# Attention scores of 16 narrow heads: from full-array contraction to two 64-row tiles of the tensor engine

## The reference

```python
# layer 0, cross attention: 248 keys (128 of the side input, 120 of the context)
q = (x1 @ Wq + bq).reshape(Bn, Nq, 16, 8).transpose(0, 2, 1, 3)
k = concat([x2 @ Wk + bk, memory_k]);  v = concat([x2 @ Wv + bv, memory_v])
attn = softmax(einsum('bhqd,bhkd->bhqk', q, k) * 8 ** -0.5)
out = einsum('bhqk,bhkd->bhqd', attn, v) ... @ Wp + bp
# layer 1, self attention: 128 keys, rotary q and k, causal mask, same 16 heads of 8
```

## Time and profile before

| what | value |
|---|---|
| median of the runs | 3703.39 us (3702.83 to 3703.52) |
| span of the profiled execution | 3703.9 us |
| PE, PEld busy | 3561.7, 3078.1 us |
| DVE, ACT, POOL busy | 2874.9, 2007.9, 1379.6 us |
| cross stage, steady | about 645 to 1573 us |
| self stage, steady | about 2390 to 2975 us |
| granted PE clock | 0.98 of full on average, 1.00 inside both narrow stages |

### The profile page before, as it was taken

The page is one execution under the profiler, slowest core; times in us unless marked ns, Lnnn a source line. Parts: engine busy times, 40 slices in busy tenths (PEclk is TensorE's granted clock), DMA queues, the critical chain, the costliest instruction groups (busy, mean ns, idle before and its releaser), DMA issues. The chain is left out here.

```text
span 3703.9 us, 96400 instructions
## 1 busy us (share of the span) xinstructions
PE 3561.7 (96%) x29010; PEld 3078.1 (83%) x29010; DVE 2874.9 (78%) x8338; ACT 2007.9 (54%) x7830; POOL 1379.6 (37%) x3847
## 2 busy tenths in 40 slices
PE   6999998999999999989999999899999989999996
PEld 5888887888888888879999999788888868888884
DVE  3777776788787888778888888677777748888887
ACT  3656664666666666622222222277777746666663
POOL 1444444444444444300000000266666624444443
PEclk8999998999999999999999999999999989999998
DMA  3000000000000000000000000000000000000000
GB/s 110 23 23 22 23 22 26 24 23 23 23 21 24 21 21 24 12 12 11 11 11 10 11 10 11 14 23 21 21 21 21 20 26 26 25 25 25 25 23 11
DMA packets 166102, 81.63 MB, mean 22 GB/s; under 512 B 19536, under 2 KB 164304, under 8 KB 165968
## 3 DMA queue, kind: packets, MB, share of 16 engines
q1 hardware_dynamic: 165968, 79.98, 7.5%
HBM read 58.94 MB, written 20.97 MB: 22 GB/s over the span
## 5 line engine op out<-in xcount | busy, mean ns | idle before, releaser
L1068 ACT ACTIVATE pr<-psS,small 128x248 f32<-128x248 f32 (+1 forms) x2048 | 838.3, 434 | 510.7 <-DVE small L1158 473.4
L1158 DVE TENSOR_REDUCE small<-psS 128x4 f32<-128x992 f32 (+1 forms) x384 | 461.1, 1201 | 215.5 <-PE psS L1030 211.9
L1283 PE MATMUL psS<-experts_xT,e 128*128 128x256 f32 x2304 | 551.4, 382 | 0.0
L1317 ACT ACTIVATE experts_th<-psS 128x512 f32<-128x512 f32 x288 | 171.9, 597 | 603.1 <-PE psS L1283 603.1
L1030 PE MATMUL psS<-cross_qk,cross_Qx 128*128 128x248 f32 x2048 | 478.8, 373 | 0.0
L1283 PEld LDWEIGHTS psS<-experts_xT,e 128*128 128x128 f32 x2304 | 416.6, 191 | 48.0
L1068 ACT ACTIVATION_READ_ACCUMULATOR pr<-psS,small 128x1 f32 x2048 | 450.7, 220 | 0.0
L985 PE MATMUL psW<-ident,pr 128*128 128x128 f32 (+1 forms) x3072 | 420.7, 280 | 5.6 <-ACT pr L1068 5.2
L985 PEld LDWEIGHTS psW<-ident,pr 128*128 128x128 f32 (+1 forms) x3072 | 328.7, 140 | 84.5 <-ACT pr L1068 44.2
L1030 PEld LDWEIGHTS psS<-cross_qk,cross_Qx 128*128 128x128 f32 x2048 | 365.4, 191 | 28.8
L819 POOL TENSOR_SCALAR pr<-pr,small 128x128 f32<-128x128 f32 (+1 forms) x1024 | 357.6, 368 | 36.4 <-DVE small L762 30.2
(11 more groups left out here) (247 smaller groups left out, 7597.0 us busy)
## 6 DMA issues: line engine op xcount, KB each, us to landing
between<-self_xo SPq DMA_DIRECT2D x128, 64.0 KB, 1.6
cross_x<-between SPq DMA_DIRECT2D x128, 64.0 KB, 1.8
cross_res<-between SPq DMA_DIRECT2D x128, 64.0 KB, 1.8
cross_cx<-in_ctx SPq DMA_DIRECT2D x128, 60.0 KB, 1.9
self_x<-in_x SPq DMA_DIRECT2D x64, 64.0 KB, 1.8
self_res<-in_x SPq DMA_DIRECT2D x64, 64.0 KB, 1.8
cross_fs<-in_fside_BxSxS SPq DMA_DIRECT2D x64, 64.0 KB, 1.9
between<-cross_xo SPq DMA_DIRECT2D x64, 64.0 KB, 1.6
```

Source lines behind the costliest of these rows:

```text
L1068: last = act.activation(pr[e.slot % 4][:, cols], K.S[e.slot % 2][:, cols], ACT.Exp, bias=nmax[e.slot % 4][:, n:n + 1], accum_out=tot[k.slo ...
L1158: dve.tensor_reduce(nmax[u.slot % 4][:], src[:, :, 0:keys], AX.X, ALU.max, negate=True).then_inc(maxed, 1)
L1283: last = pe.matmul(K.S[u.slot % 2][:, at0 + blk * T:at0 + (blk + 1) * T], w[:, j, blk * P:(blk + 1) * P], xT[i.slot][:], start=True, stop= ...
L1317: act.activation(th[u.slot % 2][:], K.S[u.slot % 2][:, 0:2 * T], ACT.Tanh, scale=0.5).then_inc(tanhed, 1)
```

## The change

Heads 0 to 7 lie on rows 0 to 63, heads 8 to 15 on rows 64 to 127. The score matmul of a head now reads only the 64 rows that hold it, of the masked q and of k. A 64-row operand uses half of the matmul array's rows: rows 0 to 63 are one row tile, rows 64 to 127 the other. Since a head needs only its half, one masked copy can hold two heads, h and h+8, and `Qx` and the mask have 8 entries instead of 16. The heads of a unit are put in order by half: the first half of a unit (one PSUM bank) comes from the upper row tile, the second half (the other bank) from the lower. `S_ps` now counts twice a unit, once for each tile. `turn_sums` is called behind all scores of the step instead of behind the first head's.

```diff
     def heads(j):
-        return [4 * g + m for m in range(j * per_unit // 4, (j + 1) * per_unit // 4) for g in range(4)]
+        ms = range(j * per_unit // 4, (j + 1) * per_unit // 4)
+        return [4 * g + m for a in range(2) for m in ms for g in (2 * a, 2 * a + 1)]
...
-        Qx = [sb(f"Qx{i}", [P, NH, P]) for i in range(2)]
+        Qx = [sb(f"Qx{i}", [P, NH // 2, P]) for i in range(2)]
...
                         for n, h in enumerate(heads(j)):
-                            if n == 1:
-                                turn_sums(u - 3)
-                            last = pe.matmul(K.S[u.slot % 2][:, n * wide:n * wide + keys], Qx[i.slot % 2][:, h, :],
-                                             qk[i.slot][:, P:P + keys], start=cross,
+                            rows = slice(64 * (h // 8), 64 * (h // 8) + 64)
+                            last = pe.matmul(K.S[u.slot % 2][:, n * wide:n * wide + keys], Qx[i.slot % 2][rows, h % 8, :],
+                                             qk[i.slot][rows, P:P + keys], start=cross,
                                              stop=cross or n % 4 == 3)
-                        last.then_inc(S_ps, 1)
-                    else:
-                        turn_sums(u - 3)
+                            if n % (per_unit // 2) == per_unit // 2 - 1:
+                                last.then_inc(S_ps, 1)
+                    turn_sums(u - 3)
...
                     if u.live:
-                        need(dve, S_ps, u.done())
+                        need(dve, S_ps, u.done(2))
...
                     if b.live:
-                        for h in heads(j):
+                        for h in heads(j)[0:per_unit // 2]:
                             last = pool.tensor_scalar(Qx[b.slot % 2][:, h, :], qk[b.slot][:, 0:P], K.headmask[:, h:h + 1],
```

More of the change, by code:

```diff
@@ L133, in allocate @@
     K.causal = K.sb("causal", [P, 4 * P], BF16)
-    K.headmask = K.sb("headmask", [P, NH])
+    K.headmask = K.sb("headmask", [P, NH // 2])
     K.rope = K.sb("rope", [P, 4 * P])
@@ L1042, in step @@
                             h, c = (heads(tj)[n // 2], n % 2) if cross else (heads(tj)[n], 0)
-                            first = tj == 0 and (n % 2 == 0 if cross else n < 4)
-                            final = tj == units - 1 and (n % 2 == 1 if cross else n >= 4)
+                            first = tj == 0 and (n % 2 == 0 if cross else n % 4 < 2)
+                            final = tj == units - 1 and (n % 2 == 1 if cross else n % 4 >= 2)
                             size = chunks[c][1]
@@ L1101, in step @@
                             need(dve, proj_ps, b.done())
-                            need(dve, S_ps, (b - 4).done(units))
+                            need(dve, S_ps, (b - 4).done(2 * units))
                             need(dve, masked, (b - 4).done(units))
@@ L1144, in step @@
                             if cross:
-                                need(dve, S_ps, (a - 4).done(units))
+                                need(dve, S_ps, (a - 4).done(2 * units))
                                 dve.tensor_copy(qk[a.slot][:, 2 * P:2 * P + CTX], W[2][:, 3 * P:3 * P + CTX])
@@ L1186, in step @@
                         need(pool, proj_sb, b.done())
-                        need(pool, S_ps, (b - 2).done(units))
+                        need(pool, S_ps, (b - 2).done(2 * units))
                     if j == 0 and n.live:
@@ L1462, in constants @@
         "c_causal": np.where(rel > 0, f(-255 * 2.0 ** 120), f(0)).astype(f),
-        "c_headmask": (np.arange(P)[:, None] // HD == np.arange(NH)[None, :]).astype(f),
+        "c_headmask": (np.arange(P)[:, None] % 64 // HD == np.arange(NH // 2)[None, :]).astype(f),
         "c_rope": np.ascontiguousarray(np.concatenate([spin[0] * gain, spin[0], spin[1] * gain, spin[1]], 1)),
```

## The result

| | before | changed |
|---|---|---|
| median of the runs | 3703.11 us (3702.83 to 3703.52) | 3730.45 us (3728.08 to 3733.61) |
| ratio, 95% interval | | 1.0076 [1.0062, 1.0090] |
| span of the profiled execution | 3703.9 us | 3729.1 us |
| cross item | 14.55 us | 14.16 us |
| self item | 9.20 us | 10.05 us |

The median of the kernel before is now that of four executions; of the three known ahead of the prediction it was 3703.39 us. The interval of the ratio lies wholly above 1, so the kernel is slower, by less than 1%.

A forecast was written before the change was run, and what follows sets the result against it. PE was taken to bound both stages, with a chain through DVE binding the cross stage after the change. Self stage +47 and cross stage -22 made +25: 3703.4 + 25 = 3728 us, range 3684 to 3762 us.

The forecast's parts named there:

- The scores: Score matmuls on PE: 1.14 instead of 1.76 us a unit in the cross stage, 1.74 instead of 1.88 in self.
- both gaps: Changes of tiling before and after a unit's cross-stage scores: 0.09 us of PE time each.
- The set-up's eight matmuls over 64 rows: Set-up trace used as model for self-stage scores: 1.34 us from first pass to start of the last.
- rival D: Row tiles run in order, one pass overlapping; nothing gained in cross scores, 0.08 us more in self; 3839 us, 6%.
- The stall: PE waits for DVE's oT ahead of the weighted sums, once an item in both stages: +0.83 us.
- the +47 of the sum: Self stage, bound by PE: items from 9.20 to 9.90 us, +45 us over 64, +47 with small waits.
- the chain of 14.17: Cross stage: chain through DVE, PE and ACT binds the item at 14.17, 14.2 us with slack; -22 us over 64 items.
- DVE's fixed order carries it on: Cross stage: projections and inputs of other items precede the maxima on DVE; only 0.35 of 2.5 us freed reaches the item.
- B: Second tile starts at once in the self stage too: scores 1.19 us, item 9.2 us; 3681 us, 13%.
- C: PE stays the cross stage's bound, DVE catching up behind the stall: item 13.0 us, about 3651 us, 8%.
- POOL's zero: POOL's 8 fewer masked copies an item change nothing, as masks are done an item ahead: zero, bounds 0 and 0.
- The register instructions added on DVE: Extra waits on S_ps, about four per cross item on DVE: 0 to 0.4 us an item, value 0.

The follow-up runs named there:

- experiment 4: Changed kernel with turn_sums called ahead of the step's scores and heads issued alternately from the two row tiles: 3599.14 us, ratio 0.9714.
- experiment 3: Changed kernel with a unit's heads issued alternately from the upper and lower row tile, turn_sums still late: 3677.41 us, ratio 0.9930.
- experiment 5: Changed kernel with all score matmuls on rows 0 to 63, one row tile instead of two: 3949.48 us, ratio 1.0660.
- Experiment 9: Changed kernel without DVE's four small context copies in the cross stage: 3728.97 us; also with ACT's copies one exponential later in one step: 3707.74 us.
- experiment 1: Changed kernel with turn_sums called ahead of the step's scores, in the self stage behind the causal mask: 3627.69 us, ratio 0.9795.
- experiment 7: Changed kernel with POOL writing 16 masked copies an item again, PE reading only eight: 3731.13 us, ratio 1.0074.
- experiment 8: Changed kernel, heads alternating, turn_sums right behind the probabilities' transposes, DVE's copy and multiplication ahead of the projections: 3592.57 us; run again, 3592.74 us.

## Why the prediction was right

**The scores.** Right in both stages. Predicted with both gaps 1.14 us in the cross stage, measured 0.10 + 1.04; in the self stage 1.74, measured 0.10 + 1.64 (2650.67 to 2652.31 in the rows below; the two mask passes take 0.43 us to a group of their own tiling in experiment 4, so they end at 2650.57). The set-up's eight matmuls over 64 rows were a fair sample of what 16 self passes would do, and experiment 3 shows that the late start of the second tile is a matter of issue order.

```profile
2650.14 0.60 PE L1027 MATMUL psS<-causal,identb 128*128 128x512 bf16 x2
2650.67 1.71 PE L1031 MATMUL psS<-self_qk,self_Qx 64*128 64x128 f32 x16
2652.31 0.66 PE L1049 MATMUL psW<-self_pT,self_Vx 128*32 128x128 f32 x16
```

Strict order of all matmuls, rival D, is out: it left nothing to gain in the cross stage, and experiment 5, where tiles cannot overlap, is 219 us over the changed kernel. The Trainium skill, page "TensorE: Matmul & The Clock Gate", section "Part 3: Packing small matmuls", says that matmuls start and end strictly in program order. The measurements disagree across the two row tiles: the sixteen self passes take 1.64 us, where rival D had 1.87 for them without the gap, and the set-up's row at 29.44 starts ahead of three matmuls issued before it.

**The stall.** Right in place and cause, a little small. Predicted +0.83 us over the gap, from 0.16 + 0.04 + 0.67 + 0.05; from the transpose's start to the weighted sums the sum made 0.06 + 0.27 + 0.04 + 0.67 + 0.05 = 1.09, the traces show 1.20 in both stages. These rows of DVE in the changed kernel hold the parts:

```profile
1004.36 0.29 DVE L1123 COPY cross_invT<-psW 128x128 f32<-128x128 f32 x1 [0.98 <-PE psW L976]
1004.76 0.29 DVE L1126 TENSOR_TENSOR cross_oT<-psW,cross_invT 128x128 f32<-128x128 f32 x1
1004.97 1.18 DVE L1160 TENSOR_REDUCE small<-psS 128x4 f32<-128x992 f32 x1
```

DVE takes 0.69 and not 0.67, and from its end (1005.05) to PE's start (1005.19) are 0.14 and not 0.05. That 0.11 an item is 7 us in the self stage, where PE is the bound: +53.9 instead of the +47 of the sum.

**The cross stage.** Right in size (-25.2 against -22, item 14.16 against 14.2), and right that the gain ends in another chain than PE's. But its terms did not all come out. The same item's later rows of DVE:

```profile
1007.63 0.29 DVE L1134 TENSOR_TENSOR cross_yb<-cross_res,rowb 128x128 f32<-128x128 f32 x1 [0.39 <-PE psW L1017]
...
1009.32 1.16 DVE L1160 TENSOR_REDUCE small<-psS 128x4 f32<-128x992 f32 x1
...
1011.05 0.34 DVE L1107 TENSOR_SCALAR cross_qk<-psW,xb 128x128 f32<-128x128 f32 x1
...
1012.30 1.18 DVE L1160 TENSOR_REDUCE small<-psS 128x4 f32<-128x992 f32 x1
```

Maxima and copies take 1.73 us (9.32 to 11.05) and not 1.93, projections 1.25 and not 1.35. In the rows of before both ended with DVE running idle, so I had counted their last instruction to its end, and an instruction right behind it starts about 0.1 us sooner; the copies had also started 0.10 us later, when PE's transposes were through. On the other side DVE's input work starts 0.36 us behind the last input transpose's pass (1007.27 to 1007.63) and not 0.20, which it is in most other items, the last maxima to the first exponential take 1.30 (1012.30 to 1013.60) and not 1.23, ACT takes 2.60 from there to the transposes (1013.60 to 1016.20) and not 2.54, and the stall was 0.11 dearer. With these the chain of 14.17 becomes 14.27 or 14.28, which is this item's length. So the rows add up to the item along this chain, but the sum made ahead of them was close because errors of 0.3 us one way and 0.4 the other nearly cancel, and that is luck.

What the sum missed altogether is the chain that runs beside it, from the maxima of an item's last unit through ACT, PE's transposes and ACT's own copies. Experiment 9 shows that DVE's chain does not set the item alone: 0.34 us less of it gave nothing. "DVE's fixed order carries it on" is therefore at best half of the truth; whether the two chains tie or the second alone is the bound stays open.

**The rivals.** B (second tile at once in the self stage) did not happen, and experiment 3 made it happen: 3677 us, where its price was 3681. C (PE stays the bound of the cross stage, item 13.0) did not happen even with the stall gone: the item was 13.5, with PE waiting for ACT (experiment 1). POOL's zero was right (experiment 7). The register instructions added on DVE were priced at nothing; no run isolates them.

**Together.** +27.3 us by the medians against +25 predicted; by stages +53.9 - 25.2 = +28.7, so 7 us more than forecast in the self stage and 3 less in the cross stage partly cancel. The cross stage's first scores also start 2.6 us earlier (645.4 to 642.8). That need not be the change's: the version of experiment 8 starts them at 643.8 us in one trace and at 645.7 in the other.

## What to carry to other kernels

When a group of work becomes shorter, or a call moves to behind it, ask what it was covering. The call that moved is one transpose of 0.11 us. Ahead of the scores its round trip through another engine was free (experiment 1); behind them it cost 0.7 us an item in the cross stage and 1.0 in the self stage, 103 us in all, more than the halved passes gave back (77 us, experiment 1 against the kernel before). For row tiles: alternate between them in program order once each has more than a few passes, and put the work of another tiling beside its like (the transpose between 64-row scores was 40 us dearer than ahead of them). This kernel also gives each tile its own PSUM bank; no run varied that.

## What the runs showed of the hardware

- fp32 matmuls on two 64-row tiles run side by side at full pace each: eight passes of 248 columns take 1.04 us, on one tile 1.86 us and over 128 rows 1.76 us. The 0.11 beyond half of 1.86 fits the first weight load and the gap at the end, about 0.2 us together, which don't shrink.
- A tile's matmuls may start ahead of another tile's that were issued before them, but only so far: 16 passes issued eight by eight take 1.64 us, issued alternately 1.09.
- Changes between 128-row and 64-row matmuls showed a gap of 0.10 us ahead of the first load (1007.27 to 1007.37, 2650.57 to 2650.67).
- PE at work almost all the time can still lose clock: with all scores on one row tile, and PE busy for 92% of the window, the self stage was granted 0.96 on average; with the same instructions on two tiles, and PE busy for 91%, it was 1.00 away from the stage's ends. Ahead of the slow stretch shown, PE had stood idle for 0.87 us, as in the items that kept their clock. Why was not tested.
